# An attention and feed-forward layer: five even query tiles, and the V projection's evacuations moved from ScalarE to VectorE

## The reference, cut to what matters

```python
mean = jnp.mean(sequence, axis=-1, keepdims=True)
var = jnp.mean(jnp.square(sequence - mean), axis=-1, keepdims=True)
x = (sequence - mean) / jnp.sqrt(var + EPS) * ln_gamma + ln_beta
q, k, v = (_split_heads(x @ W.T + b) ...)          # 16 heads of 64
scores = jnp.einsum('bhqd,bhkd->bhqk', q, k) / scale
scores = jax.nn.sigmoid(scores - mu) * jnp.exp(scores)
scores = scores / jnp.sum(scores, axis=-1, keepdims=True)
out = jnp.einsum('bhqk,bhkd->bhqd', scores, v) ... @ Wo.T + bo
...
x = _layernorm(x + attention(x))
x = _layernorm(x + ffn(x))      # r = sigmoid(xr W_r), k = relu(xk W_k)^2, r * (k W_v)
```

## Time and profile before

| | us |
|---|---|
| median of 2 runs, slowest core | 6674.2 (6671.5 to 6676.9) |
| the profiled execution | 6668.8 |
| its span, first to last instruction, core 7 | 6667.2 |
| spans of the 8 cores | 6646.9 to 6667.2 |

### The profile page before, as it was taken

The page is one execution under the profiler, slowest core; times in us unless marked ns, Lnnn a source line. Parts: engine busy times, 40 slices in busy tenths (PEclk is TensorE's granted clock), DMA queues, the critical chain, the costliest instruction groups (busy, mean ns, idle before and its releaser), DMA issues.

```text
span 6667.2 us, 68688 instructions; the slowest of 8 cores (6646.9 to 6667.2 us)
## 1 busy us (share of the span) xinstructions
PE 4690.8 (70%) x15252; PEld 1241.5 (19%) x15252; DVE 3320.9 (50%) x3578; ACT 4840.4 (73%) x5925; POOL 824.6 (12%) x1540
## 2 busy tenths in 40 slices
PE   2687777767777776777777677767767777775544
PEld 0232224531111111111111111111111111111212
DVE  2000001346666665666666566666656666665342
ACT  0444445779999995999999499999959999993111
POOL 2234333210000000000000000000000000000111
PEclk7799887555555556555555555555565555556677
DMA  7212222421111111111111111111111110110111
GB/s 222 81 56 79 80 89 83 121 81 32 31 30 32 32 42 32 32 32 30 32 32 43 31 32 32 31 31 32 32 42 32 32 32 30 32 32 31 63 63 63
DMA packets 182632, 332.78 MB, mean 50 GB/s; under 512 B 37354, under 2 KB 119274, under 8 KB 182260
## 3 DMA queue, kind: packets, MB, share of 16 engines
q0 software_dynamic: 73664, 185.17, 8.4%
q1 hardware_dynamic: 108596, 143.22, 7.3%
HBM read 277.39 MB, written 50.86 MB: 49 GB/s over the span
## 4 chain that ended last, share of the span: by engine, by line
ACT 50%; PE 18%; issue 12%; DVE 12%; DMA 5%; POOL 1%; ACTq 1%; DVEq 0%; POOLq 0%; SPq 0%
ACT tbf L872 35%; ACT ebf L875 11%; DVE wbf L989 5%; PE pr_ps L1300 3%; PE o_ps L973 2%; PE pjp L480 2%; PE st_ps L941 2%; DMA ktd<-ktev 2%; DVE dinvb L1006 1%; PE ktp L515 1%; PE o_ps L977 1%; PE pp L1099 1%; ACT xntk L669 1%; ACT xntk L671 1%; POOL vd L495 1%
## 5 line engine op out<-in xcount | busy, mean ns | idle before, releaser
L989 DVE SCALAR_TENSOR_TENSOR wbf<-tbf,ebf 128x1024 bf16<-128x1024 bf16 (+1 forms) x2560 | 2592.2, 1014 | 1810.9 <-ACT ebf L875 1750.8
L872 ACT ACTIVATE tbf<-st_ps,mubc 128x1024 bf16<-128x1024 f32 (+1 forms) x2560 | 2948.5, 1152 | 345.1 <-PE st_ps L945 216.4
L875 ACT ACTIVATE ebf<-st_ps,ln2b 128x1024 bf16<-128x1024 f32 (+1 forms) x2560 | 2956.0, 1155 | 0.0
L973 PE MATMUL o_ps<-wbf,vbx 128*65 128x512 bf16 (+1 forms) x2560 | 1321.5, 516 | 1153.6 <-DVE wbf L989 1121.2
L977 PE MATMUL o_ps<-wbf,vbx 128*65 128x512 bf16 (+1 forms) x2560 | 1371.9, 536 | 0.0
L941 PE MATMUL st_ps<-qt_sb,ktb 64*128 64x512 bf16 (+1 forms) x2560 | 1295.2, 508 | 83.4 <-ACT ebf L875 74.7
L945 PE MATMUL st_ps<-qt_sb,ktb 64*128 64x512 bf16 (+1 forms) x2560 | 1311.3, 515 | 0.0
L905 POOL DMA_DIRECT2D ktb<-ktd x640 | 343.1, 536 | 4355.9 <-PE st_ps L945 4277.6
L973 PEld LDWEIGHTS o_ps<-wbf,vbx 128*65 128x65 bf16 x2560 | 333.9, 130 | 2222.0 <-issue 2193.0
L941 PEld LDWEIGHTS st_ps<-qt_sb,ktb 64*128 64x128 bf16 x2560 | 253.1, 100 | 1696.4 <-issue 1672.0
L977 PEld LDWEIGHTS o_ps<-wbf,vbx 128*65 128x65 bf16 x2560 | 394.3, 154 | 0.0
(11 more groups left out here) (192 smaller groups left out, 2456.7 us busy)
## 6 DMA issues: line engine op xcount, KB each, us to landing
vbx<-vd SPq DMA_DIRECT2D x640, 132.0 KB, 2.1
ktb<-ktd POOLq DMA_DIRECT2D x640, 128.0 KB, 2.3
xg<-xkv SPq DMA_DIRECT2D x64, 512.0 KB, 5.3
vd<-vev POOLq DMA_DIRECT2D x512, 33.0 KB, 2.3
ktd<-ktev POOLq DMA_DIRECT2D x128, 128.0 KB, 2.0
woh_sb<-wos POOLq DMA_DIRECT2D x80, 128.0 KB, 2.5
xq<-xkv SPq DMA_DIRECT2D x16, 512.0 KB, 5.2
wch<-wrs POOLq DMA_DIRECT2D x32, 256.0 KB, 3.2
```

What stands on the lines that cost most here:

```text
L872: ac.inc(s.activation(tbuf[k % WBUF][:].rearrange("p (h w) -> p h w", h=2)[:, :, 0:W], srcv, AF.Tanh, bias=mubc[:], scale=0.5))
L875: a2.inc(s.activation(ebuf[k % WBUF][:].rearrange("p (h w) -> p h w", h=2)[:, :, 0:W], srcv, AF.Exp, bias=ln2b[:], scale=1.0))
L973: tn.matmul(o_ps[par][0][0:65, 0:W], vb[c2 % 4][:, 132 * j:132 * j + 65], wbuf[k2 % WBUF][:, 0:W], start=(k2 == 0), stop=(k2 == KS - 1))
L989: s1.inc(v.scalar_tensor_tensor(vw(wbuf[k % WBUF][:]), vw(tbuf[k % WBUF][:]), 1.0, vw(ebuf[k % WBUF][:]), op0=AX.add, op1=AX.mult))
```

## The change

Two edits, independent of each other.

1. `qt_widths` divides the query columns evenly: for 2049 columns [410, 410, 410, 410, 409] in place of [1, 512, 512, 512, 512]. All of the attention follows from this list: tile widths, offsets, and the number of 128-row blocks in `emit_xt_prep` (for the first tile four in place of one).
2. The V evacuations (two per token tile, PSUM to `v_ev`) leave ACT's program. A new `emit_vevac` puts them on DVE, after the projection of the same token tile in the program, so on DVE's queue after the norms of group g and before the chain of group g+1. PE's wait for a free V bank is for the evacuation that used this bank last, and `emit_vstore` waits for DVE.

```diff
 def qt_widths(nq):
-    ws = []
-    rem = nq
-    while rem > 512:
-        ws.append(512)
-        rem -= 512
-    ws.append(rem)
-    return [ws[-1]] + ws[:-1]
+    n = (nq + 511) // 512
+    base = nq // n
+    extra = nq - base * n
+    return [base + 1] * extra + [base] * (n - extra)
...
                         for hf in range(2):
-                            idx = 2 * t + hf
-                            bk = idx % 3
-                            if idx >= 3:
-                                tn.wait_ge(ac.sem, vVEa[(idx - 3) // 2])
+                            bk = (2 * t + hf) % 3
+                            if bk in last_pj_evac:
+                                tn.wait_ge(dv.sem, last_pj_evac[bk])
...
+                def emit_vevac(t):
+                    @blk.vector
+                    def _(v, t=t):
+                        for hf in range(2):
+                            bk = (2 * t + hf) % 3
+                            v.wait_ge(pe.sem, pV[t] - (1 - hf))
+                            if t >= 2:
+                                v.wait_ge(dVs[t % 2].sem, gV[t - 2])
+                            dst = v_ev[t % 2][:, 4 * hf:4 * (hf + 1), :].rearrange(
+                                "p a (h x) -> p a h x", h=2)[:, :, :, 0:64]
+                            src = pj_ps[bk][:].rearrange("p (a h x) -> p a h x",
+                                                         a=4, h=2)
+                            ins = v.tensor_copy(dst, src)
+                            dv.inc(ins)
+                            last_pj_evac[bk] = dv.v
+                            v.wait_ge(dv.sem, dv.v)
+                        vVE[t] = dv.v
+
                 def emit_vstore(t):
                     @blk.gpsimd
                     def _(g, t=t):
-                        g.wait_ge(ac.sem, vVEa[t])
+                        g.wait_ge(dv.sem, vVE[t])
...
                 @blk.scalar
                 def _(s):
-                    def emit_vevacs_act(s, gp):
-                        for t in range(4 * gp, 4 * gp + 4):
-                            for hf in range(2):
-                                bkp = (2 * t + hf) % 3
-                                s.wait_ge(pe.sem, pVv[t] - (1 - hf))
-                                if t >= 2:
-                                    s.wait_ge(dVs[t % 2].sem, gVv[t - 2])
-                                dst = v_ev[t % 2][:, 4 * hf:4 * (hf + 1), :].rearrange(
-                                    "p a (h x) -> p a h x", h=2)[:, :, :, 0:64]
-                                srcp = pj_ps[bkp][:].rearrange(
-                                    "p (a h x) -> p a h x", a=4, h=2)
-                                ch(s, ac, s.activation(dst, srcp, AF.Identity))
-                            assert ac.v == vVEa[t]
                     for g in range(NG4):
-                        if g >= 1:
-                            emit_vevacs_act(s, g - 1)
                         for t in range(4 * g, 4 * g + 4):
...
-                    emit_vevacs_act(s, NG4 - 1)
                     emit_ktq_evacs(s, NG4 - 1)
...
                     for tt2 in range(4 * g, 4 * g + 4):
                         emit_vproj(tt2)
+                        emit_vevac(tt2)
                         emit_vstore(tt2)
```

More of the change, by code:

```diff
@@ L499, in _ @@
                         gV[t] = dVs[t % 2].v
-                        assert dVs[t % 2].v == gVv[t]
                 def emit_ktproj(hh):
@@ L593, in build @@
                         pVv[t] = cpx
+                        cvx += 2
                     hh = g
@@ L602, in build @@
                 cax = acB
-                vVEa = {}
                 for g in range(NG4):
-                    if g >= 1:
-                        for t in range(4 * (g - 1), 4 * (g - 1) + 4):
-                            cax += 2
-                            vVEa[t] = cax
                     for t in range(4 * g, 4 * g + 4):
@@ L626, in build @@
                         vEa[t] = cax
-                for t in range(4 * (NG4 - 1), 4 * (NG4 - 1) + 4):
-                    cax += 2
-                    vVEa[t] = cax
                 hp2 = NG4 - 1
```

## The result

The changed kernel takes 6511.7 us (median of 9 runs, 6496.6 to 6580.1), the kernel before 6673.3 beside it. The ratio is 0.974, with a 95% interval of 0.971 to 0.977. The longest execution had the cores of one die at a granted clock of 0.57 where all others had 0.58 to 0.59, and the ratio goes by the executions without that. The forecast was 6441: the kernel is faster, by 162 us where 233 were forecast. The profiled execution has a span of 6507.2 us on core 7 (6492.3 to 6507.2 over the cores) and took 6509.0.

A forecast was written before the change was run, and what follows sets the result against it. ACT was taken to bound the 512-column tiles, the order of work the projection phase. Span 6667.2 - 125 (tiles) + 11 (preparation) - 119 (projection) = 6434 us, with 7 above the span 6441; range 6395 to 6535.

The forecast's parts named there:

- projection: Projection phase: V evacuations moved to DVE shorten groups with and without Q; gain 119 us.
- preparation: Before the first tile: four transposed input blocks instead of one, first tanh 19 us after 1091 instead of 8; cost 11 us.
- tiles: Attention: five even tiles of 983 us, 4908 us in all against 5033 before; gain 125 us.
- The iteration: Attention loop at 410 columns: ACT's tanh and exp set the pace, 0.828 us each, 1.655 us per key block.
- What is in a tile besides the stream: Tile period outside the key blocks (head changes, output projection, layer norm): 136 us at 410 columns, by a line.
- Rival 1: Attention loop: the dependency chain sets the pace at 410 columns; up to 125 us more, 6566; chance 0.10.
- a load takes some 5 us more: Before the first tile: load time added to the 14.3 us of preparation, from the xq median of 5.2 us.
- from there each pair of K evacuations waits for a landing: Projection group after the first K store: 4.02 us per landing, third K evacuation at 31, eighth about 40.
- in the four groups with Q the stores are hidden by the Q projection: Projection phase, groups with Q: 59.5 us against 68.1, gain 8.6 x 4 = 34 us.
- Rival 2: Projection phase gains little because POOL holds it, V evacuations on DVE delaying V and K stores; 6560 us; chance 0.10.
- Rivals 3: Attention loop: the iteration doesn't fall with tile width, since fixed-length steps fill it; 868 us more, 7309; chance 0.02.
- rival 4: Projection phase runs at PE's pace, 41.3 us per group; 35 to 45 us less, 6400; chance 0.04.

The follow-up runs named there:

- third block of lag: AV issued three key blocks behind the scores instead of two: 6458.9 us on the changed kernel, 6557.8 us on the kernel before.
- second run: The changed kernel itself, unchanged, run again as a control beside three other kernels: 6556.9 us, ratio 0.984.
- third run: The changed kernel, unchanged, once more with the last runs of the study: 6539.7 us, ratio 0.982.
- token loads late: Changed kernel with the loads of a group's four token tiles held back until the sixth K evacuation: 6504.5 us, ratio 0.976.
- 28 issues fewer: Changed kernel with each token tile's V stored by one DMA of 264 KB instead of eight of 33 KB: 6546.4 us, ratio 0.980.
- combined kernel: Changed kernel with AV three blocks behind, the 127-row load cut into 112 and 15 rows, and token loads held back: 6400.1 us, ratio 0.960.
- split load: Changed kernel with the first tile's load of 127 rows sent as two loads, 112 and 15 rows: 6525.1 us, ratio 0.978.

## Why the prediction was right, and by how much it missed

The direction and the two mechanisms were right, and so was the place of the waits in the groups without Q. The wait that stays in the groups with Q, and the long landing ahead of the first tile, were not foreseen. 6511.7 lies in the range of 6395 to 6535, and the forecast was 71 us too low. That it lies in the range is in part luck: on the two later occasions the same kernel took 6556.9 and 6539.7, above the range, because its projection phase was some 40 us longer. In the profiled execution the misses by term are 24 (projection), 20 (preparation), 17 (tiles), and 11 (feed-forward, spread between cores).

- **The iteration.** Forecast 0.828 for an ACTIVATE of 820 elements, measured 0.827. The straight line through 2, 512 and 1024 elements held. Mis-sized is the step that took the shortest sequence of before, 1.994, as the mean: it was 2.003 there, and after the mean is 1.670 in place of 1.655. 0.015 x 2560 = 38 us. Both means are away from the changes of heads.
- **What is in a tile besides the stream.** Forecast 136, measured 986 - 512 x 1.670 = 131 us, which gives 25 us back. Periods were 978 to 990 against 983. The tiles brought 96.2 + 11.5 = 108 us where 125 were forecast.
- **Rival 1** (1.704 by the chain) did not come. The tanh group after stands 195.5 us for scores, all of it within the first 16 blocks after a change of heads; in the other 48 blocks the profile shows no idle time of ACT, only slips (1.670 against 1.655). So the sign of being wrong, idle time inside the loop, showed at the changes of heads alone, as in the wide tiles of the kernel before. But a chain through PE does cost some 90 to 110 us in both kernels, as the third block of lag shows. The sentence "ACT has no idle time between its instructions at 512 columns" was read from five iterations; the groups of all 2560 show more. Of the kernel before:

```profile
L872 ACT ACTIVATE tbf<-st_ps,mubc 128x1024 bf16<-128x1024 f32 (+1 forms) x2560 | 2948.5, 1152 | 345.1 <-PE st_ps L945 216.4 <-DVE wbf L989 106.7 <-issue 0.3
...
L973 PE MATMUL o_ps<-wbf,vbx 128*65 128x512 bf16 (+1 forms) x2560 | 1321.5, 516 | 1153.6 <-DVE wbf L989 1121.2 <-issue 8.2
```

PE stood before AV for 1121.2 us there. This row would have led to the largest gain that one edit brought in these runs.
- **The preparation.** Forecast +11, measured +31.4. The failed term is "a load takes some 5 us more": it priced a transfer of 127 rows by the median of transfers of 128 rows. Such a shape did not exist in the kernel before. All else in that step held within half a microsecond.
- **The projection phase.** Forecast against measured, medians over the groups without Q, us from the first V projection:

| | forecast | after | second run | third run | token loads late |
|---|---|---|---|---|---|
| last V evacuation ends | 19.5 | 20.7 | 18.8 | 18.3 | 19.5 |
| first K evacuation starts | 21.5 | 22.8 | 20.8 | 20.4 | 21.6 |
| first K store | 27 | 26.6 | 24.6 | 24.1 | 24.9 |
| third K evacuation | 31 | 32.2 | 35.4 | 34.9 | 29.2 |
| eighth K evacuation | 40 | 41.4 | 44.4 | 44.1 | 40.1 |
| next group | 44.5 | 45.2 | 48.1 | 47.9 | 44.2 |

With the token loads out of the way the group goes as the prediction wrote it. The failed step is "from there each pair of K evacuations waits for a landing": it took the 4 us of the earlier trace rows, where the moved work has put token loads beside the stores, and there it takes 6.0 to 10.4 us from the first K store to the third K evacuation (medians of the three profiles). I had counted the DMAs of the V stores and K stores, and not those that the earlier norms release. Second, "in the four groups with Q the stores are hidden by the Q projection": a stall in the K projections stands before Q and nothing makes it up. PE still waited 21.8 us in the four groups for K evacuations; measured 63.3 for 59.5, and 58.7 with the late loads.
- **Rival 2** (projection gains little, POOL holds it) was half right in its result, 6560, and wrong in its cause. Repeated, the changed kernel took 6556.9 and 6539.7, near it; but 28 issues fewer for each group brought nothing, and the CASTs on DVE hold POOL hardly at all: a V store issue took 569 ns in the mean against 538. The Trainium skill's rules, cited in the prediction, that a two-port mode of DVE locks POOL (SBUF — State Buffer, "Who interferes with whom") and that a PSUM operand excludes this mode (VectorE: DVE Perf Modes, "Why PSUM operands drop a tier") agree with that.
- **Rivals 3 and 4** did not occur. The 41.3 us of rival 4 was not reached as a mean by any core of any run; the lowest was 43.8.

Two things stay open. Why the crowd makes a group 45 us long on one occasion and 48 on another isn't settled; the three later occasions used a different chip each, so the chip isn't excluded as the reason. And the combined kernel's groups, 45 to 48 with the same late loads that gave 44 to 47 in their own run, show that the stores can still be late.

## What to carry to other kernels

When an edit moves work earlier, list every transfer that the moved work releases, and lay those beside the stores that the next evacuations wait for; a wait on the load queue is a cheap cure, and here it was worth more than the choice of queue for the stores. Price a transfer by a row of the same shape; one of 127 rows was a new shape here, not a slightly smaller one. And before a loop is called bound by one engine, read the idle time of the *other* engines' groups over the whole loop: what stands queued behind a wait on PE showed up only there.

## What the runs showed of the hardware

The cores of a die are not independent in the projection phase. Landings in the changed kernel by core, here cores 6 and 7 of the third run (count, KB each, median us to landing):

```profile
xg<-xkv SPq DMA_DIRECT2D x64, 512.0 KB, 6.6
vd<-vev POOLq DMA_DIRECT2D x512, 33.0 KB, 4.4
```

```profile
xg<-xkv SPq DMA_DIRECT2D x64, 512.0 KB, 10.8
vd<-vev POOLq DMA_DIRECT2D x512, 33.0 KB, 2.7
```

On core 6 the V stores are slow and the token loads fast, on core 7 the other way round. It is so in each of the pairs 0 and 1, 2 and 3, 4 and 5, 6 and 7, in four profiles of this order (the first and the two later ones of the changed kernel, and that with the split load), 16 pairs of 16: the core that issues its token loads earlier, counted from the start of its own span, by 5.4 to 11.7 us in the median over the groups, has the long token loads (medians of 8.2 to 10.8 us, its partner 5.8 to 7.8), and its partner has the long V stores (2.9 to 4.7 us against 2.1 to 3.4). The two cores of a pair also have nearly the same group time, as 45.9 and 45.7 on cores 4 and 5 of the first profile, or 47.1 and 46.8 on cores 0 and 1 beside 43.8 and 44.1 on cores 6 and 7 with the late loads. That last difference goes with the granted clock of the pairs, 0.84 and 0.86 against 0.93 from 480 to 960 us, more than with their transfers. In the kernel before, loads took 5.3 to 5.8 us on every core. From the landings it looks as if neighbours share something on the way of their transfers, and the loads of one meet the stores of the other; how far they are apart would then decide the cost, which would explain why it changes from one occasion to the next. This is only a reading of the traces, with offsets taken from each core's own start; no run was made that sets the offset.

A load of 127 rows moved at 23 to 28 GB/s and took 25 us; its 112 and 15 rows as two transfers took 5.1.
